# Relative attention: the placing products write PSUM in adjacent words, and ScalarE's copies of them read PSUM by a stride

## The chip, the core and the metric

The kernel is one program on one core of a Trainium2 chip. The core has five engines with queues of their own: TensorE (matrix products, shown as PE, its weight loads as PEld), VectorE (DVE), ScalarE (ACT), GpSimd (POOL) and SyncE (SP, here the main issuer of DMAs). Products land in PSUM, an accumulator memory of eight banks with 512 words of 32 bits on each of 128 partitions; everything else lies in SBUF. The metric is the device time of one execution in microseconds.

## The reference

Four blocks follow each other, each added to x (16 sequences of 256 tokens, 256 features) through a gate: causal attention, a feed-forward block with ternary weights, an attention with relative positions, and a mixture of 64 experts. The change lies in the third. Cut to it, with 16 heads of d = 16, and P = 128:

```python
qh = heads(layernorm(x) @ Wq.T + bq); kh = heads(ctx @ Wk.T + bk); vh = heads(ctx @ Wv.T + bv)
qk = einsum('bhqd,bhkd->bhqk', qh, kh)
r_k = rk_table[clip(k - q, -P, P) + P]          # one row of d for each pair (q, k)
q_rk = einsum('bhqd,qkd->bhqk', qh, r_k)
attn = softmax((qk + q_rk) / sqrt(d))
w1 = einsum('bhqk,bhkd->bhqd', attn, vh)
w2 = einsum('bhqk,qkd->bhqd', attn, r_v)        # r_v like r_k, from rv_table
x = x + tanh(g) * (rows(w1 + w2) @ Wo.T + bo)
```

The term q_rk differs for each query, so it is a product for each query over all heads, while qk is a product for each head over all queries.

## The kernel before

`relative_attention` takes four sequences at a time with all their heads (64 heads in all, `BH`), in four quarters of 64 queries (`CQ`), which makes 16 half-steps. One iteration h of `run` works on two of them: the *front* of half-step h + 1 (its scores and the shift for the softmax) and the *back* of half-step h (exponentials and weighting), and for some h also the *tail* of h - 1 (adding w1 and w2, dividing, the output product) and the projection of the next two sequences. On TensorE an iteration has three stretches.

1. The **front stretch**, a loop over 16 chunks c. Each chunk has 8 **placing products** (line 1444), one for each query q: the weights are 128 columns of the table `rk6` from column j on, the moving operand is `q_now[:, :, q]`, 64 heads of one query, that lie 64 bf16 numbers apart. The output goes to one of two banks `ps_s`. In the kernel before it lands with the 8 queries of a chunk side by side for each head, so the 64 words of one product are 8 words apart. ScalarE copies a chunk's 512 words to the tile `score` (line 1315, through its view `by_query`), where a query's scores of one head stand side by side. The second chunk of a bank waits for the copy of the first (`place_copied`). After every second chunk there are 4 **spreading products** (line 1455), which lay the shift of half-step h out in `ps_t`; VectorE adds it to the scores of half-step h (line 1204, `take_shift`) and ScalarE takes their exponential (line 1302, `take_exp`). In ScalarE's queue an exponential stands behind every second copy from the fourth on, and the last two exponentials stand behind the last copy. Where the iteration has a projection, its transposes and products lie between the chunks (`project`), and ScalarE and VectorE take them out of PSUM between their own steps. Where it has a tail in this stretch (`late == 0`), the tail lies at chunks 8 to 14 and waits for GpSimd's sum of w1 and w2 (line 1098).
2. The **score stretch**, again 16 chunks: 8 scoring products for a chunk (line 1475), one for each head over 64 adjacent queries, written in adjacent words; VectorE adds them to the placed part in `score` (line 1225). Between them are the first weighting's products (line 1497), four at a time in four column tiles of the array. In the other iterations the tail lies here (`late == 1`).
3. The **key stretch**: the maximum over keys, by transposes (line 1512), and the **second weighting** (line 1524): for each query a product over all heads, with a moving operand read by stride and an output written by stride, four at a time in column tiles.

The expert block, behind it, has one more line that the prediction reads: the **map products** (line 1890), whose weights and moving operand are read by a stride of 64 bf16 numbers and whose output is written in adjacent words.

Two lines hold the access patterns in question:

```python
pe.matmul(ps_s[c % 2][:].rearrange("p (h q) -> p q h", h=BH)[:, n, :], rk6[:, j:j + P], q_now[:, :, q], ...)
act.activation(by_query[1 - par][:, c // 8, :, q0:q0 + 8], ps_s[c % 2][:].rearrange("p (h q) -> p h q", h=BH), ACT.Copy)
```

Of the kernel before, what the change touches and what calls it, by code (L numbers as in the profile page):

```python
# [11 lines left out]
ACT = mybir.ActivationFunctionType  # L12
AX = mybir.AxisListType

P = 128
# [777 lines left out]
def relative_attention(nc, x2, ctx, g_xattn, w_q, b_q, w_k, b_k, w_v, b_v, w_o, b_o, rk_t, rv_table, x3, pack, rv_ext):  # L793
# [18 lines left out]
    BH = NB * H  # L812
# [12 lines left out]
    with ExitStack() as stack:  # L825
# [4 lines left out]
        def sem(name):  # L830
            sems.append(nc.alloc_semaphore("r_" + name))
            return sems[-1]
# [8 lines left out]
        rk6 = sb("rk6", [PR, NJ], BF16)  # L841
# [28 lines left out]
        ps_s = [pb(f"ps_s{i}", [P, 512], F32) for i in range(2)]  # L870
# [15 lines left out]
        placed, place_copied, scored, added = sem("placed"), sem("place_copied"), sem("scored"), sem("added")  # L886
# [15 lines left out]
        def fill_at(c):  # L902
            if c < CH:
                return c - 2 if c >= 2 else None
            return CH - 2 + (c - CH) // 2 if c % 2 == 0 and c < CH + 8 else None
# [347 lines left out]
        def _(act):  # L1253
# [36 lines left out]
            def step(h, front, back, tail, project_next):  # L1290
                i, t = divmod(h, 4)
                u, par, late = NP * (i + 1) + t, h % 2, t // NP

                def copy_rows():
                    act.wait_ge(z_turned, START + (h - 1) + 1)
                    act.activation(attT.rearrange("p (e s q) -> p s e q", e=2, s=NB), TAIL_BANKS[late][0][:].rearrange("p (s e q) -> p s e q", s=NB, e=2),
                                   ACT.Copy).then_inc(z_copied, 1)

                def take_exp(m):
                    act.wait_ge(shifted, START + MC * h + m + 1)  # L1300
                    part = score[par][:, :, 4 * m:4 * m + 4, :].rearrange("p k h q -> p k (h q)")
                    act.activation(part, part, ACT.Exp, scale=float(DH) ** -0.5).then_inc(expd, 1)  # L1302

                if project_next:
                    act.wait_ge(projected, START + u * FILLS - PER_BATCH + QK)
                    act.dma_start(ctx_in[:], c_rows[u, 0]).then_inc(ctx_loaded, 16)
                    act.dma_start(x_in[:], x_rows[u, 0]).then_inc(x_loaded, 16)
                for c in range(CH):
                    if front:

                        act.wait_ge(placed, START + CH * (h + 1) + c + 1)
                        if c == 0 and back:
                            act.wait_ge(w2_done, START + 2 * h)
                        q0 = 8 * (c % 8)
                        act.activation(by_query[1 - par][:, c // 8, :, q0:q0 + 8],  # L1315
                                       ps_s[c % 2][:].rearrange("p (h q) -> p h q", h=BH), ACT.Copy).then_inc(place_copied, 1)
                    if back and c % 2 and c > 1:
                        take_exp(c // 2 - 1)
                    if tail and late == 0 and c == TAIL_SLOTS[0][1]:
                        copy_rows()  # L1320
                    if project_next and c >= 2:
                        project(u, fill_at(c), h + 1)
                if back:
                    take_exp(MC - 1)
                if project_next:
                    for f in range(CH - 2, FILLS):
                        project(u, f, h + 1)
                if tail and late == 1:
                    copy_rows()
                if back:  # L1330
                    for n in range(2):
                        act.wait_ge(av_done, START + 2 * h + n + 1)
                        if n == 0:
                            act.wait_ge(att_turned, START + 2 * h)
                        act.activation(avT[:, 8 * n:8 * n + 8, :].rearrange("p g q -> p (g q)"), ps_b[n][:],
                                       ACT.Copy).then_inc(av_copied, 1)
                    for n in range(2):
                        act.wait_ge(w2_done, START + 2 * h + n + 1)
                        if n == 0:
                            act.wait_ge(av_added, START + h)  # L1340
                        act.activation(w2_raw[:, :, :, 8 * n:8 * n + 8],
                                       ps_b[n][:].rearrange("p (j g q) -> p j g q", j=4, g=NG), ACT.Copy).then_inc(w2_copied, 1)

            run(step)

        @block.tensor
        def _(pe):
# [49 lines left out]
            def step(h, front, back, tail, project_next):  # L1397
# [3 lines left out]
                q_now = q6[(h + 1) % 2]  # L1401
# [29 lines left out]
                for c in range(CH):  # L1431
                    if front:

                        if c == 0:
                            for n in range(2):
                                pe.wait_ge(packed_q[n], START + 48 * (h + 1) + 48)
                        if c == 0:
                            pe.wait_ge(added, START + CH * (h + 1))
                        if c >= 2:
                            pe.wait_ge(place_copied, START + CH * (h + 1) + c - 1)  # L1440
                        for n in range(8):
                            q = 8 * (c % 8) + n
                            j = (c // 8) * P - (q_first + q) + S - 1
                            ins = pe.matmul(ps_s[c % 2][:].rearrange("p (h q) -> p q h", h=BH)[:, n, :], rk6[:, j:j + P], q_now[:, :, q],  # L1444
                                            start=True, stop=True)
                        ins.then_inc(placed, 1)
                    if back and c % 2:

                        m = c // 2
                        if m == 0:  # L1450
                            pe.wait_ge(shift_ready, START + 2 * h + 2)
                        if m >= 2:
                            pe.wait_ge(shifted, START + MC * h + m - 1)
                        for n in range(4):
                            ins = pe.matmul(ps_t[m % 2][:, n * P:(n + 1) * P],  # L1455
                                            pick_row[:, 4 * m + n:4 * m + n + 1].to_broadcast([2 * HC, P]),
                                            shift[:], start=True, stop=True)
                        ins.then_inc(spread, 1)
                    if tail and late == 0:
                        take_tail(c)  # L1460
                    if project_next and c >= 2:
                        project(u, fill_at(c), h - 1 if tail else None)
                for c in range(CH):
                    if project_next and fill_at(CH + c) is not None:
                        project(u, fill_at(CH + c))
                    if front:
# [7 lines left out]
                        for n in range(8):  # L1474
                            ins = pe.matmul(ps_s[c % 2][:, n * CQ:(n + 1) * CQ], k6[:, h0 + n, k * P:(k + 1) * P],  # L1475
                                            q_now[:, h0 + n, :], start=True, stop=True)
# [3 lines left out]
                    if back:  # L1480
# [12 lines left out]
                        for k in range(NT):  # L1493
                            for j in range(4):
                                hd = 4 * g + j
                                first = (k * BH + hd) * VC
                                ins = pe.matmul(ps_b[g // 8][32 * j:32 * j + 32, (g % 8) * CQ:(g % 8 + 1) * CQ],  # L1497
                                                v_all[:, first:first + 32], by_query[par][:, k, hd, :],
                                                start=(k == 0), stop=(k == NT - 1), skip_group_check=True,
                                                tile_position=(0, 32 * j))  # L1500
                        if g % 8 == 7:
                            ins.then_inc(av_done, 1)
                for c in range(MC):
                    if front:
# [6 lines left out]
                        for n in range(4):  # L1511
                            ins = pe.transpose(ps_t[c % 2][:, n * P:(n + 1) * P], key_max[c % 2][:, n * P:(n + 1) * P], ident[:])  # L1512
                        ins.then_inc(turned, 1)
                    if back:
# [3 lines left out]
                        for n in range(2 * c, 2 * c + 2):  # L1518
                            for k in range(NT):
                                for j in range(4):  # L1520
                                    q = NQ * j + n
                                    m = k * P + S - 1 - (back_first + q)
                                    out = ps_b[n // 8][32 * j:32 * j + 32, :].rearrange("p (j g q) -> p q g j", j=4, g=NG)[:, n % 8]
                                    ins = pe.matmul(out, rv[:, m * DH:m * DH + 32], by_query[par][:, k, :, q],  # L1524
                                                    start=(k == 0), stop=(k == NT - 1), skip_group_check=True,
                                                    tile_position=(0, 32 * j))
                        if c % 4 == 3:
                            ins.then_inc(w2_done, 1)
                if front:
# [3 lines left out]
                        .then_inc(max_turned, 1)  # L1533

            run(step)

    nc.clear_and_free_semaphores(sems)
# [602 lines left out]
```

## Time and profile before

| | us |
|---|---|
| median of 3 runs | 2696.76 (2685.21 to 2705.37) |
| the profiled execution | 2701.31 |
| its span, first to last instruction | 2699.5 |
| TensorE busy with products | 2007.7 (74%) |
| VectorE busy | 1284.3 (48%) |
| ScalarE busy | 835.6 (31%) |
| placing products, line 1444, 2048 of them | 254.7 |
| copies of them, line 1315, 256 of them | 152.8 |

The mean granted clock of TensorE was 0.809 of full speed. Busy shares are means over stages with different limits; a change inside one stage is read from that stage's own windows and timeline. Records of products are pipelined: one lasts longer than the distance to the next, so the distance between starts is the pace.

### The profile page before, as it was taken

What the parts mean: (1) busy time and instruction counts of PE and PEld (TensorE: products, weight loads), DVE (VectorE), ACT (ScalarE), POOL (GpSimd) and SP (SyncE); (2) the same over time, 40 slices, a digit from 0 to 9 for tenths busy, and PEclk for the clock granted to TensorE, in tenths of its full rate; (3) what the DMA queues carried; (4) which work ended last, traced back from release to release, by engine and by line L of the source; (5) the groups of instructions that cost most, each with busy time, mean ns of one, the idle gap of its engine ahead of it and who ended that gap; (6) DMA issues with size and microseconds to landing.
All of it is one profiled execution on the core that took longest, in us unless ns stands there. A gap on an engine that the chain in (4) does not pass through costs nothing. (4 is left out here: it accounts for less than half of the span.)

```text
span 2699.5 us, 54675 instructions
## 1 busy us (share of the span) xinstructions
PE 2007.7 (74%) x22307; PEld 1513.8 (56%) x22308; DVE 1284.3 (48%) x2419; ACT 835.6 (31%) x1484; POOL 559.6 (21%) x519
## 2 busy tenths in 40 slices
PE   4777777774677458999999999989647757776663
PEld 3545554453566346777777777777535535554442
DVE  3434444442777216666666656656437642111112
ACT  2333333331222123434443443344224531111110
POOL 1111111110000101101110110001010008888881
PEclk8889888887788767987987887777857779888985
DMA  4455445543021452232224222311012225566566
GB/s 91 84 95 90 84 87 95 93 85 85 27 70 63 130 102 45 64 65 52 64 56 80 65 60 48 57 29 29 21 51 68 68 63 130 117 128 127 127 115 194
DMA packets 272334, 216.38 MB, mean 80 GB/s; under 512 B 88740, under 2 KB 257166, under 8 KB 271616
## 3 DMA queue, kind: packets, MB, share of 16 engines
q1 hardware_dynamic: 238528, 179.01, 29.2%
q0 software_dynamic: 24576, 27.05, 6.0%
q10 hardware_dynamic: 9024, 7.35, 0.9%
q8 instruction: 156, 2.56, 0.4%
q14 instruction: 50, 0.41, 0.1%
HBM read 147.08 MB, written 72.45 MB: 81 GB/s over the span
## 5 line engine op out<-in xcount | busy, mean ns | idle before, releaser
L1444 PE MATMUL r_ps_s<-r_q,r_rk 96*128 96x64 bf16 x2048 | 254.7, 289 | 15.0 <-DMA r_q<-parts_scratch 15.0
L1444 PEld LDWEIGHTS r_ps_s<-r_q,r_rk 96*128 96x128 bf16 x2048 | 217.4, 120 | 38.2 <-issue 29.0
L1204 DVE TENSOR_TENSOR r_score<-r_score,r_ps_t 128x1024 f32<-128x1024 f32 x128 | 154.8, 1217 | 100.4 <-PE r_ps_t L1455 100.4
L1315 ACT ACTIVATE r_score<-r_ps_s 128x512 f32<-128x512 f32 x256 | 152.8, 597 | 151.1 <-PE r_ps_s L1444 150.4
L1225 DVE TENSOR_TENSOR r_score<-r_ps_s,r_score 128x512 f32<-128x512 f32 x256 | 171.5, 688 | 53.6 <-PE r_ps_s L1475 51.3
L2001 DVE TENSOR_TENSOR e_hT<-e_sil,e_ps_gu 128x256 f32<-128x256 f32 x64 | 26.9, 421 | 324.6 <-ACT e_sil L2023 324.6
L313 DVE TENSOR_REDUCE a_row_max<-a_ps_s 128x2 f32<-128x512 f32 (+1 forms) x192 | 127.6, 685 | 66.1 <-PE a_ps_s L478 59.4
L1962 POOL DMA_INDIRECT e_rows<-rows_w_scratch,k_token x128 | 135.0, 1055 | 99.5 <-DVE e_h_last L1989 60.6
L2030 ACT ACTIVATE e_y<-e_ps_y,e_rows 128x256 f32<-128x256 f32 x128 | 53.7, 471 | 326.1 <-DMA base_scratch<-e_y,k_token 167.0
L1524 PE MATMUL r_ps_b<-r_score,r_rv 128*32 128x64 f32 x4096 | 137.9, 288 | 10.9 <-issue 10.9
L1302 ACT ACTIVATE r_score<-r_score 128x1024 f32<-128x1024 f32 x128 | 134.5, 1051 | 20.2 <-DVE r_score L1204 19.6
L1098 POOL TENSOR_TENSOR r_avT<-r_avT,r_w 128x1024 f32<-128x1024 f32 x16 | 37.6, 2353 | 494.3 <-DMA r_w<-r_w_raw 494.3
L1475 PE MATMUL r_ps_s<-r_q,r_k 96*128 96x64 bf16 x2048 | 114.0, 203 | 27.3 <-DVE r_score L1225 14.2
L2068 PE MATMUL e_ps_last<-e_wd,e_h_last 128*64 128x256 f32 x128 | 44.8, 435 | 115.0 <-DVE e_h_last L2002 114.0
L399 ACT ACTIVATE a_p<-a_ps_s 128x512 f32<-128x512 f32 x192 | 106.7, 595 | 74.0 <-PE a_ps_s L524 35.4
L1524 PEld LDWEIGHTS r_ps_b<-r_score,r_rv 128*32 128x32 f32 x4096 | 105.2, 126 | 35.0 <-issue 35.0
L1242 DVE TENSOR_REDUCE r_row_max<-r_ps_t 128x4 f32<-128x512 f32 x128 | 88.5, 691 | 66.6 <-PE r_ps_t L1512 66.4
L1497 PE MATMUL r_ps_b<-r_score,r_v_all 128*32 128x64 f32 x4096 | 116.8, 239 | 0.0
L1475 PEld LDWEIGHTS r_ps_s<-r_q,r_k 96*128 96x128 bf16 x2048 | 83.8, 104 | 58.6 <-DVE r_score L1225 19.4
L478 PE MATMUL a_ps_s<-a_k,a_q 96*128 96x256 bf16 (+1 forms) x512 | 102.8, 306 | 13.2 <-DVE a_row_max L313 11.6
L786 PE MATMUL f_ps_out<-f_w_q,f_h_hi 128*128 128x256 f32 x256 | 76.6, 329 | 41.0 <-DVE f_h_lo L712 41.0
L1977 POOL DMA_INDIRECT slots_in_scratch<-e_y,k_token x64 | 102.4, 1600 | 19.6 <-issue 18.9
(295 smaller groups left out, 4277.4 us busy)
## 6 DMA issues: line engine op xcount, KB each, us to landing
a_q<-parts_scratch SPq DMA_DIRECT2D x96, 128.0 KB, 4.2
a_k<-parts_scratch SPq DMA_DIRECT2D x96, 128.0 KB, 4.3
r_q<-parts_scratch SPq DMA_DIRECT2D x96, 128.0 KB, 3.2
e_wg<-in_L_ffn_expert_wg SPq DMA_DIRECT2D x64, 128.0 KB, 2.5
e_wu<-in_L_ffn_expert_wu SPq DMA_DIRECT2D x64, 128.0 KB, 3.0
e_wd<-in_L_ffn_expert_wd SPq DMA_DIRECT2D x64, 128.0 KB, 3.4
r_k<-parts_scratch SPq DMA_DIRECT2D x4, 1536.0 KB, 14.1
rows_w_scratch<-m_row SPq DMA_DIRECT2D x8, 640.0 KB, 3.2
```

What stands on the lines that cost most here:

```text
L313: dve.tensor_reduce(row_max[:, t, h0:h0 + n], ps_s[c % 2][:].rearrange("p (h k) -> p h k", h=n), AX.X, ALU.max).then_inc(maxed, 1)
L399: act.activation(out.rearrange("p h q -> p (h q)"), ps_s[c % 2][:], ACT.Exp).then_inc(expd, 1)
L478: ins = pe.matmul(out[:, h, :], q6[par][0:PR, h0 + h, t * P:(t + 1) * P], k6[par][0:PR, h0 + h, 0:keys], start=(t == 1), stop=(t == 0), sk ...
L1204: dve.tensor_tensor(part, part, bcast(ps_t[m % 2][:], NT), ALU.add).then_inc(shifted, 1)
L1225: dve.tensor_tensor(part, ps_s[c % 2][:], part, ALU.add).then_inc(added, 1)
L1302: act.activation(part, part, ACT.Exp, scale=float(DH) ** -0.5).then_inc(expd, 1)
L1315: act.activation(by_query[1 - par][:, c // 8, :, q0:q0 + 8], ps_s[c % 2][:].rearrange("p (h q) -> p h q", h=BH), ACT.Copy).then_inc(place_ ...
L1444: ins = pe.matmul(ps_s[c % 2][:].rearrange("p (h q) -> p q h", h=BH)[:, n, :], rk6[:, j:j + P], q_now[:, :, q], start=True, stop=True)
L1475: ins = pe.matmul(ps_s[c % 2][:, n * CQ:(n + 1) * CQ], k6[:, h0 + n, k * P:(k + 1) * P], q_now[:, h0 + n, :], start=True, stop=True)
L1497: ins = pe.matmul(ps_b[g // 8][32 * j:32 * j + 32, (g % 8) * CQ:(g % 8 + 1) * CQ], v_all[:, first:first + 32], by_query[par][:, k, hd, :], ...
L1524: ins = pe.matmul(out, rv[:, m * DH:m * DH + 32], by_query[par][:, k, :, q], start=(k == 0), stop=(k == NT - 1), skip_group_check=True, ti ...
L1962: pool.indirect_dma_start(out=rows[u][:, c, :], out_offset=None, in_=rows_w, in_offset=bass.IndirectOffsetOnAxis(ap=token[:, e * C + c:e * ...
```

## The change

Inside a bank of `ps_s` the order of a placed chunk is turned: it was head by head with the 8 queries side by side, and becomes query by query with the 64 heads side by side. A placing product now writes 64 adjacent words, and ScalarE's copy reads words 64 apart (256 bytes) with its output order unchanged. The scoring products, which use the same banks later, and the second weighting stay as they are.

```diff
@@ ScalarE, front stretch
-                                       ps_s[c % 2][:].rearrange("p (h q) -> p h q", h=BH), ACT.Copy).then_inc(place_copied, 1)
+                                       ps_s[c % 2][:].rearrange("p (q h) -> p h q", h=BH), ACT.Copy).then_inc(place_copied, 1)
@@ TensorE, front stretch
-                            ins = pe.matmul(ps_s[c % 2][:].rearrange("p (h q) -> p q h", h=BH)[:, n, :], rk6[:, j:j + P], q_now[:, :, q],
+                            ins = pe.matmul(ps_s[c % 2][:, n * BH:(n + 1) * BH], rk6[:, j:j + P], q_now[:, :, q],
                                             start=True, stop=True)
```

## Rows read from the trace of the kernel before

**Rows 1.** Windows: the relative attention (columns: stretch, length, busy by engine, clock, DMA)

```profile
979.50:1903.00 923.50, 841.85 (x13210) 670.00 (x13214) 564.35 (x863) 358.57 (x592) 98.58 (x92) 0.81 0.28 57
```

**Rows 2.** Windows of front stretches: first, projection, plain, tail

```profile
979.50:1006.50 27.00, 14.35 (x128) 13.07 (x128) 0.00 (x0) 9.56 (x16) 0.00 (x0) 0.50 0.79 127
...
1332.80:1367.50 34.70, 32.47 (x231) 26.54 (x230) 17.08 (x34) 22.50 (x42) 7.63 (x8) 0.90 0.42 99
1400.80:1419.80 19.00, 19.00 (x161) 15.90 (x160) 9.12 (x9) 15.09 (x23) 3.63 (x2) 0.59 0.23 57
...
1754.20:1783.60 29.40, 25.04 (x182) 20.76 (x182) 11.07 (x14) 15.44 (x24) 3.60 (x2) 0.59 0.17 45
```

**Rows 3.** Timeline of one chunk pair in a plain front stretch

```profile
1405.37 1.94 PE L1444 MATMUL r_ps_s<-r_q,r_rk 96*128 96x64 bf16 x16
...
1407.24 0.60 PE L1455 MATMUL r_ps_t<-r_shift,r_pick_row 64*128 64x128 bf16 x4
1407.34 0.60 ACT L1315 ACTIVATE r_score<-r_ps_s 128x512 f32<-128x512 f32 x1 [0.29 <-PE r_ps_s L1444]
...
1407.77 1.94 PE L1444 MATMUL r_ps_s<-r_q,r_rk 96*128 96x64 bf16 x16
1407.84 1.05 ACT L1302 ACTIVATE r_score<-r_score 128x1024 f32<-128x1024 f32 x1
...
1408.86 0.60 ACT L1315 ACTIVATE r_score<-r_ps_s 128x512 f32<-128x512 f32 x1
```

**Rows 4.** Lines by form, TensorE and ScalarE (busy us, mean ns, idle before)

```profile
L1444 PE MATMUL r_ps_s<-r_q,r_rk 96*128 96x64 bf16 x2048 | 254.7, 289 | 15.0 <-DMA r_q<-parts_scratch 15.0
...
L1315 ACT ACTIVATE r_score<-r_ps_s 128x512 f32<-128x512 f32 x256 | 152.8, 597 | 151.1 <-PE r_ps_s L1444 150.4
L1524 PE MATMUL r_ps_b<-r_score,r_rv 128*32 128x64 f32 x4096 | 137.9, 288 | 10.9 <-issue 10.9
...
L1302 ACT ACTIVATE r_score<-r_score 128x1024 f32<-128x1024 f32 x128 | 134.5, 1051 | 20.2 <-DVE r_score L1204 19.6
L1497 PE MATMUL r_ps_b<-r_score,r_v_all 128*32 128x64 f32 x4096 | 116.8, 239 | 0.0
L1475 PE MATMUL r_ps_s<-r_q,r_k 96*128 96x64 bf16 x2048 | 114.0, 203 | 27.3 <-DVE r_score L1225 14.2 <-DMA r_k<-parts_scratch 12.7
...
L2023 ACT ACTIVATE e_sil<-e_ps_gu 128x256 f32<-128x256 f32 x64 | 24.6, 384 | 34.3 <-PE e_ps_gu L2059 34.3
```

**Rows 5.** Lines by form, VectorE: a strided read and a plain pass

```profile
L1731 DVE TENSOR_REDUCE m_recent<-m_mask 128x64 f32<-128x256 bf16 x8 | 4.7, 593 | 0.0
...
L1708 DVE TENSOR_SCALAR m_logit<-m_ps_lp 128x256 f32<-128x256 f32 x8 | 3.3, 415 | 6.4 <-PE m_ps_lp L1847 6.4
```

**Rows 6.** Windows of the placing products alone, at either clock

```profile
1400.80:1402.60 1.80, 1.80 (x16) 1.62 (x16) 1.00 0.09 18
1407.80:1409.60 1.80, 1.80 (x16) 1.64 (x16) 0.50 0.12 27
```

**Rows 7.** Windows of the map products alone, at either clock

```profile
2203.60:2206.10 2.50, 2.50 (x120) 2.50 (x124) 0.50 0.33 116
2206.40:2208.90 2.50, 2.50 (x124) 2.50 (x116) 1.00 0.18 59
```

**Rows 8.** Timeline of TensorE: the first weighting at either clock

```profile
1420.35 0.66 PE L1497 MATMUL r_ps_b<-r_score,r_v_all 128*32 128x64 f32 x16
...
1429.06 0.43 PE L1497 MATMUL r_ps_b<-r_score,r_v_all 128*32 128x64 f32 x16
```

**Rows 9.** Windows of all engines at these two times (clock behind POOL)

```profile
1420.30:1420.90 0.60, 0.60 (x19) 0.42 (x16) 0.60 (x1) 0.60 (x1) 0.00 (x0) 0.50 0.00 0
1429.10:1429.40 0.30, 0.30 (x18) 0.23 (x16) 0.22 (x2) 0.30 (x1) 0.00 (x0) 1.00 0.00 0
```

**Rows 10.** TensorE's waits in the relative attention

```profile
PE r_ps_s L1475 <- DMA r_k<-parts_scratch: 12.7, 1, 12.7
...
PE r_ps_b L1415 <- POOL r_avT L1098: 8.7, 3, 4.4
```

## The prediction

> **What bounds the kernel now.** I first look for the stage that the edit lies in. The windows view gives the relative attention 923.5 us of the 2699.5, with TensorE busy in 841.85 of them and ScalarE in 358.57 [rows 1]. The placing products (L1444) run in its front stretches, sixteen in all, one for each front half-step. Both edited lines lie in these, so the next view is one window for each kind of stretch [rows 2]. There are four kinds. The very first (27.0 us) has no other work beside it. Six carry a projection of the next sequences (31.4 to 36.0 us; the one shown 34.7). Seven have neither a projection nor a tail (18.8 to 19.0 us; the one shown 19.00, TensorE busy in every microsecond of it). Two have a tail alone (28.5 and 29.4 us). The timeline of one pair of chunks in the third kind then shows what is late [rows 3]: TensorE starts 16 placing products at 1405.37, four spreading products at 1407.24 and the next 16 at 1407.77, so a pair takes 2.40 us without a gap on TensorE. ScalarE does two copies and one exponential in it, and stands idle 0.29 us ahead of the second copy. So TensorE sets the pair, with ScalarE close behind; VectorE has half of the stretch free (busy 9.12 of 19.00 us [rows 2]).
>
> How much room ScalarE has comes from the same rows. Its instructions overlap a little: a copy of 0.60 us is followed 0.50 us after its start (1407.34 to 1407.84), an exponential of 1.05 us 1.02 us after its start (1407.84 to 1408.86). A chunk that starts at 1407.77 has its copy started at 1408.86, 1.09 us later. In a stretch, 15 copies and 6 exponentials stand before the last copy starts (the exponentials of a chunk pair run one pair late, the last two behind the last copy). If ScalarE alone set the pace, that would be 1.09 + 15 x 0.50 + 6 x 1.02 = 14.7 us, against the 19.0 of TensorE. Reckoned back, copies can grow until 1.09 + 15 x (d - 0.10) + 6.12 = 19.0, that is to d = 0.89 us from 0.597 [rows 4], before they set this kind of stretch.
>
> **What the change does, part by part.** No instruction, wait, DMA or semaphore is added, removed or moved; only two access patterns in PSUM change. 2048 products write 64 adjacent words in place of 64 words that lie 8 words apart, and 256 copies read words 64 apart in place of adjacent ones. Their output in SBUF keeps its order.
>
> *The products.* They start 16 in 1.87 us, 0.117 us each [rows 3]. The scoring products (L1475) have the same shape, with adjacent words on both sides, and take 114.0 us for 2048, 56 ns each, against 254.7 and 124 [rows 4]. So something in the placing products costs 68 ns each. Three things differ: the weights start at odd places of a table, the moving operand is read by a stride of 128 bytes (q_now[:, :, q]), and the output is written by a stride. The change takes away the third alone. What tells them apart:
> - The second weighting (L1524) also reads its moving operand and writes PSUM by stride, but has 32 adjacent weights like the first weighting (L1497); it takes 137.9 us against 116.8 [rows 4]. So odd weights are not needed for a loss, but this row doesn't part the read from the write.
> - The map products of the next stage (L1890) do. They read moving operand and weights by a stride of 128 bytes and write PSUM in adjacent words, half as many columns as L1497. In 2.5 us there are 120 of them at clock 0.50 and 124 at clock 1.00, 20 to 21 ns each at either [rows 7]. The first weighting, with nothing strided, follows the clock: 16 in 0.66 us at a clock of 0.50, 0.43 at 1.00 [rows 8, 9]. A strided read of SBUF alone therefore makes TensorE's pace independent of its clock, as it is in L1444. (What stays open is whether the strided weights do it here, which L1444 doesn't have, or the strided operand, which it has.)
> - VectorE shows a price for the same kind of read: a reduction that reads 256 elements by a stride of 128 bytes takes 593 ns, a plain pass over 256 elements 415 [rows 5]. That is 0.70 ns an element more, on an engine that has nothing to do with TensorE's clock.
>
> So the strided read is enough to explain the placing products' pace, and it stays. Bounds for the gain: 0 (the read sets the pace), and 68 ns each, down to the scoring products. A loss is out: nothing is added on TensorE. I take 0, by the nearest rows, L1890's and the reduction's.
>
> *The copies.* No row shows ScalarE reading PSUM, or anything, by such a stride. Its own pace bounds the price from below: 384 ns for 256 and 597 for 512 elements [rows 4], 0.83 ns an element and 171 ns fixed; from SBUF it is the same (1024 elements in 1051 ns), so a changed read can't gain. From above, two rows on hops give an estimate each: VectorE's 0.70 ns more an element makes 597 + 512 x 0.70 = 0.95 us, and TensorE's placing pace of 117 ns for 64 elements, 1.83 ns each, makes 171 + 512 x 1.83 = 1.11 us. I take 597 with no conviction: all rows on hops are reads of SBUF, and none on PSUM. But up to 0.89 us the third kind of stretch does not notice, and there the cover is the 4.3 us between 14.7 and 19.0. In the first stretch placing ends in any case before the keys land (12.7 us of waiting for that DMA), and in the two stretches with a tail TensorE waits 8.7 us in all for GpSimd's sum [rows 10]; in the six with a projection ScalarE is busy for 22.50 of 34.70 us [rows 2], so 16 x 0.29 = 4.6 us more have room, if the projection's own chain through ScalarE does not lengthen. What a longer copy holds up, when it does, is the queue behind it on ScalarE: the exponentials, and in six stretches the projection's copies, for which TensorE and VectorE wait.
>
> **The sum.** 0 from the products, 0 from the copies: the profiled execution stays at 2701.3 us (span 2699.5). It stood 4.5 us over the median of the three runs, so the forecast is 2697.
>
> **Rivals.**
> *A, faster: the write was the brake.* For it: placing and second weighting share it. Against it: L1890. Then TensorE drops below ScalarE, and the seven plain stretches come down only to 14.7 us: 7 x 4.3 = 30. The six with a projection, where TensorE is busy in 32.47 of 34.70 us, gain at most 16 chunks x (0.93 - 0.45) = 8, I take 5: 30. (A chunk is 8 products: 0.93 us at 117 ns, 0.45 at 56.) The two with a tail gain on the 7 chunks behind the wait, 7 x 0.48, 3 each: 6. 2697 - 66 = 2631. The Trainium skill (PSUM — Partial Sum Buffer, Specifications (TRN2)) says that PSUM has cachelines of 8 bytes and that any non-contiguous access slows matmuls significantly; by that rule this rival is what happens. No run here shows a strided write with an adjacent read, so the rule stands untested, and L1890 shows only that it is not needed.
>
> *B, slower: the copies' strided read costs what it costs from SBUF.* A copy of 1.03 us, between the two estimates, starts its follower 0.93 later; a plain stretch takes 1.09 + 15 x 0.93 + 6.12 = 21.2 us, 2.2 more, 15 in seven. In the six with a projection the 16 x 0.43 = 6.9 us of longer copies lie partly in idle time; between 0 and 6.9 each, I take 1.5: 9. The two with a tail 0.5 each. 2697 + 25 = 2722. At 0.95 us a plain stretch takes 20.0 and the six nothing: 2704. At 1.11 us it takes 22.4 and the six up to 8.2 each: 2770. It decides from a copy of 0.89 us on. For it: both engines that hop in SBUF pay. Against it: PSUM is another memory, and it takes 64 adjacent words from TensorE in 56 ns, faster than ScalarE asks for them. The Trainium skill (Advanced Engine Details and Errata, PSUM Cachelines) asks that every two consecutive elements be adjacent for the best throughput, which speaks against a copy that never has two; no row here shows it for ScalarE.
>
> *C, both or dearer:* A's gain eaten by B's copies (plain stretches at 21.2 us although TensorE has time, the projection stretches shorter: 2697 + 15 - 30 = 2682 to 2712), or a hop dearer than either estimate: a copy of 1.45 us makes a plain stretch 27.5, 60 us more in seven, near 2760 without the six.
>
> **How the numbers follow.** Nothing that counts: 0.48, in 2686 to 2708 by the spread of the runs shown. B: 0.33. A: 0.12. C: 0.07. One per cent, 27 us, is about what a measurement of this kernel can tell from no change. B straddles that line (2704 to 2770, the line at 2724), so I give 0.20 of it to slower, the longer arm, and 0.13 to within. C gives 0.05 to slower and 0.02 to within. Slower is 0.25; faster is A, 0.12; within is 0.48 + 0.13 + 0.02 = 0.63. The range leaves out A (0.12) and the top of B and C (some 0.08): 2682 to 2750.
>
> **What the changed profile would show.** Right: L1444 still 16 in about 1.87 us, at either clock; L1315 below 0.89 us; the plain stretches at 18.8 to 19.0. A: L1444's busy time near the 114 of L1475, TensorE waiting for ScalarE's copies. B: L1315 between 0.95 and 1.11 us, idle time ahead of L1444 released by L1315, plain stretches near 21.2. The forecast is wrong if a hop in PSUM has a price of its own that SBUF rows can't show.

## The result and the profile after

The changed kernel takes 2714.79 us (median of 17 runs, 2706.31 to 2726.68) against 2694.93 of the kernel before on the same chips (17 runs): a ratio of 1.0073, 95% interval 1.0059 to 1.0087. That is 19.9 us slower, inside the range forecast and within 1%, but not nothing. The profiled execution took 2723.16 us with a mean granted clock of 0.787, against 2701.31 and 0.809 before.

Both edited lines kept their prices. The view by lines and forms of the kernel after has the rows that answer to [rows 4] (busy us, mean ns, idle before):

```profile
L1444 PE MATMUL r_ps_s<-r_q,r_rk 96*128 96x64 bf16 x2048 | 255.1, 288 | 14.9 <-DMA r_q<-parts_scratch 14.9
L1524 PE MATMUL r_ps_b<-r_score,r_rv 128*32 128x64 f32 x4096 | 138.0, 288 | 11.4 <-issue 11.4
L1497 PE MATMUL r_ps_b<-r_score,r_v_all 128*32 128x64 f32 x4096 | 121.9, 247 | 0.0
L1475 PE MATMUL r_ps_s<-r_q,r_k 96*128 96x64 bf16 x2048 | 119.3, 208 | 25.6 <-DMA r_k<-parts_scratch 12.8 <-DVE r_score L1225 12.3
...
L1315 ACT ACTIVATE r_score<-r_ps_s 128x512 f32<-128x512 f32 x256 | 152.9, 597 | 153.9 <-PE r_ps_s L1444 153.4
```

The placing products (L1444) and their copies (L1315) stand where they stood. What grew are lines that the change does not touch, in the same number of products: the projection's (L1379, two forms) by 11.0 us in all, the scoring products (L1475) and the first weighting (L1497) by 5 us each. The projection's lines, before and then after:

```profile
L1379 PE MATMUL r_ps_proj<-r_xT,r_wq_dh 128*128 128x256 f32 x128 | 45.9, 510 | 2.2 <-ACT r_xT L1276 2.2
L1379 PE MATMUL r_ps_proj<-r_cT,r_wk_dh 128*128 128x256 f32 x128 | 38.7, 429 | 0.6 <-DVE r_rest L1162 0.4
...
L1379 PE MATMUL r_ps_proj<-r_xT,r_wq_dh 128*128 128x256 f32 x128 | 53.0, 573 | 1.9 <-ACT r_xT L1276 1.9
L1379 PE MATMUL r_ps_proj<-r_cT,r_wk_dh 128*128 128x256 f32 x128 | 42.6, 466 | 0.4 <-DVE r_rest L1162 0.4
```

All of these follow TensorE's clock. At the median, projection products start 216 ns apart at a granted clock of 1.00 and 427 at 0.50, scoring products 29 and 53, the same in both kernels; for the first weighting see [rows 8, 9]. So what changed is how long each level lasted, and the next view is the windows by stretch, whose last three columns are the granted clock, the DMA share and GB/s. After, a projection stretch, a plain stretch, a stretch with a tail alone and the score stretch behind it:

```profile
1098.10:1134.19 36.09, 34.99 (x229) 28.63 (x229) 17.05 (x34) 22.71 (x42) 7.71 (x8) 0.76 0.42 95
1468.60:1487.61 19.01, 19.01 (x162) 15.92 (x161) 9.11 (x9) 15.10 (x23) 2.37 (x1) 0.56 0.44 69
...
1763.60:1793.27 29.67, 24.92 (x181) 20.75 (x181) 11.07 (x14) 15.46 (x24) 3.61 (x2) 0.60 0.18 45
1793.27:1812.11 18.84, 17.31 (x387) 13.28 (x385) 12.94 (x19) 3.57 (x5) 0.00 (x0) 0.55 0.07 17
```

The plain and the tail-only stretch are as before [rows 2]. The score stretch of the last row had this form before:

```profile
1783.56:1796.66 13.10, 11.35 (x387) 8.95 (x385) 12.78 (x19) 3.58 (x5) 0.00 (x0) 1.00 0.11 24
```

There VectorE was busy nearly throughout (12.78 of 13.10 us); after, TensorE at half clock sets it. Cutting both traces at the first placing and the first scoring product of each half-step gives the whole bill: the six projection stretches take 215.0 us against 203.8, the two score stretches behind the tail-only ones 37.9 against 26.2, and the relative attention, from its first placing to its last weighting product, 990.2 against 968.0. These two places hold 22.9 us, all of the 22.2.

One projection stretch cut where its clock changes shows how. Windows of before (the same stretch of both kernels, the second of the six):

```profile
1094.01:1100.31 6.30, 5.06 (x45) 4.14 (x45) 2.93 (x8) 2.81 (x6) 0.00 (x0) 1.00 0.35 106
1100.31:1107.11 6.80, 6.32 (x38) 4.92 (x37) 3.11 (x5) 4.64 (x9) 1.89 (x2) 0.50 0.18 41
1107.11:1127.77 20.66, 20.59 (x150) 17.38 (x148) 11.02 (x22) 14.99 (x28) 5.82 (x7) 1.00 0.53 119
```

and of after:

```profile
1098.10:1102.40 4.30, 3.23 (x29) 2.64 (x28) 1.79 (x3) 1.97 (x4) 0.00 (x0) 1.00 0.51 144
1102.40:1119.40 17.00, 16.97 (x96) 13.37 (x96) 7.42 (x15) 9.99 (x19) 5.66 (x5) 0.50 0.33 77
1119.40:1134.19 14.79, 14.79 (x107) 12.63 (x105) 7.84 (x16) 10.76 (x20) 2.05 (x3) 1.00 0.49 101
```

The clock falls to its lower level 4.3 us into the stretch in place of 6.3, and stays there for 17.0 us in place of 6.8. TensorE's busy time grows by 3.0 us (31.97 to 34.99), 0.7 of which go into its idle time, and the stretch is 2.3 us longer. TensorE's timeline in these spells shows which work pays. Before, at 1.00:

```profile
1108.50 1.13 PE L1379 MATMUL r_ps_proj<-r_xT,r_wq_dh 128*128 128x256 f32 x4
1109.47 1.06 PE L1444 MATMUL r_ps_s<-r_q,r_rk 96*128 96x64 bf16 x8
```

After, at 0.50:

```profile
1109.34 2.08 PE L1379 MATMUL r_ps_proj<-r_xT,r_wq_dh 128*128 128x256 f32 x4
1111.21 1.08 PE L1444 MATMUL r_ps_s<-r_q,r_rk 96*128 96x64 bf16 x8
```

Four projection products take twice the time, eight placing products the same. So the placing products, whose pace does not follow the clock, lose nothing by the lower clock; what stands beside and behind them does.

### The profile page after: what moved, and what is told of

It reads as the page before. It is cut to its first block and busy times, and to the rows that moved or that the text cites. A ratio compares the mean times of both kernels' runs of the same rounds, so it can differ in the third digit from the quotient of the medians.

```text
span 2721.4 us, 54676 instructions
## 1 busy us (share of the span) xinstructions
PE 2043.0 (75%) x22308; PEld 1539.4 (57%) x22308; DVE 1284.5 (47%) x2419; ACT 837.0 (31%) x1484; POOL 560.2 (21%) x519
## 5 line engine op out<-in xcount | busy, mean ns | idle before, releaser
L1444 PE MATMUL r_ps_s<-r_q,r_rk 96*128 96x64 bf16 x2048 | 255.1, 288 | 14.9 <-DMA r_q<-parts_scratch 14.9
L1444 PEld LDWEIGHTS r_ps_s<-r_q,r_rk 96*128 96x128 bf16 x2048 | 219.3, 121 | 41.4 <-issue 33.1
L1315 ACT ACTIVATE r_score<-r_ps_s 128x512 f32<-128x512 f32 x256 | 152.9, 597 | 153.9 <-PE r_ps_s L1444 153.4
L1524 PE MATMUL r_ps_b<-r_score,r_rv 128*32 128x64 f32 x4096 | 138.0, 288 | 11.4 <-issue 11.4
L1475 PE MATMUL r_ps_s<-r_q,r_k 96*128 96x64 bf16 x2048 | 119.3, 208 | 25.6 <-DMA r_k<-parts_scratch 12.8
L1524 PEld LDWEIGHTS r_ps_b<-r_score,r_rv 128*32 128x32 f32 x4096 | 105.2, 127 | 36.4 <-issue 36.4
L1497 PE MATMUL r_ps_b<-r_score,r_v_all 128*32 128x64 f32 x4096 | 121.9, 247 | 0.0
L1475 PEld LDWEIGHTS r_ps_s<-r_q,r_k 96*128 96x128 bf16 x2048 | 88.2, 107 | 58.8 <-DVE r_score L1225 17.5
```

What stands on the lines that cost most here:

```text
L1444: ins = pe.matmul(ps_s[c % 2][:, n * BH:(n + 1) * BH], rk6[:, j:j + P], q_now[:, :, q], start=True, stop=True)
```

## The experiments

All ratios are against the kernel before on the same chip. Where a line is not shown, it is that of the changed kernel (or of the kernel before, if that is named). "Plain", "projection" and "tail-only" are the kinds of front stretch. The clocks of the six projection stretches stand in order. Times of stretches and clocks are those of one profiled execution each, the ratios those of all runs.

| run | placing write | projection, us in all | their clocks | score stretches behind the tail-only ones | ratio [interval] |
|---|---|---|---|---|---|
| before | stride | 203.8 | .76 .90 .90 .90 .90 .81 | 26.2 | 1 |
| read strided alone | stride | 202.9 | .76 .90 .95 .86 .90 .90 | 26.2 | 0.9999 [0.9983, 1.0015] |
| adjacent in plain alone | by kind | 202.9 | .77 .90 .90 .86 .90 .90 | 26.2 | 1.0011 [0.9997, 1.0025] |
| after | adjacent | 215.0 | .65 .76 .76 .80 .73 .72 | 37.9 | 1.0073 [1.0059, 1.0087] |
| write adjacent alone | adjacent | 214.0 | .65 .80 .76 .81 .73 .72 | 37.4 | 1.0082 [1.0059, 1.0105] |
| adjacent in projection and tail | by kind | 211.9 | .65 .76 .76 .81 .76 .75 | 37.5 | 1.0067 [1.0042, 1.0092] |
| pairs | pairs | 214.5 | .65 .80 .81 .72 .73 .72 | 26.2 | 1.0064 [1.0041, 1.0086] |

**The two halves of the change.** In the first of these runs the products write adjacent words and ScalarE reads adjacent words, in the second both go by stride.

```diff
@@ write adjacent alone (against after)
-  ps_s[c % 2][:].rearrange("p (q h) -> p h q", h=BH), ACT.Copy)
+  ps_s[c % 2][:].rearrange("p (h q) -> p h q", h=BH), ACT.Copy)
@@ read strided alone (against before)
-  ps_s[c % 2][:].rearrange("p (h q) -> p h q", h=BH), ACT.Copy)
+  ps_s[c % 2][:].rearrange("p (q h) -> p h q", h=BH), ACT.Copy)
```

> The placing products write adjacent words as in the changed kernel, ScalarE's copies read adjacent words as in the kernel before (the scores of a chunk then land in another order in SBUF, so the output is another one; every instruction has its old size). Theory 'clock': the write pattern has no price on TensorE (16 placing products still in 1.87 us) but lets the granted clock fall in the front stretches, so this is as slow as the changed kernel: ratio 1.006 to 1.009, mean clock near 0.79. Theory 'copies': ScalarE's strided read disturbs something that its own duration doesn't show; then this equals the kernel before, ratio 0.998 to 1.002, clock near 0.81.

> The placing products write by stride as in the kernel before, ScalarE's copies read by stride as in the changed kernel (order in SBUF and so the output differ). Theory 'clock': equals the kernel before, ratio 0.998 to 1.002, copies at 597 ns, clock near 0.81. Theory 'copies': ratio 1.006 to 1.009.

The write alone gave the whole loss, the read alone nothing: 2711.57 us (1.0082) and 2689.04 (0.9999). Lines by form of the second:

```profile
L1315 ACT ACTIVATE r_score<-r_ps_s 128x512 f32<-128x512 f32 x256 | 152.9, 597 | 150.5 <-PE r_ps_s L1444 149.8
```

A ScalarE copy that reads PSUM 64 words apart takes 597 ns, like one that reads adjacent words. So the loss is the write's, with ScalarE's pattern out of it. Windows of the first run, a projection stretch and a score stretch behind a tail-only one, show it at the same places as in the changed kernel:

```profile
1091.91:1126.45 34.54, 34.04 (x230) 27.94 (x229) 17.17 (x34) 22.68 (x42) 7.66 (x8) 0.80 0.43 99
1779.83:1798.44 18.61, 17.08 (x386) 13.09 (x385) 12.85 (x19) 3.57 (x5) 0.00 (x0) 0.56 0.07 17
```

**The operand made adjacent, under either write.** The moving operand takes one head's 64 queries, which lie side by side, in place of one query's 64 heads.

```diff
@@ with the adjacent write of after; and with the strided write of before
-  rk6[:, j:j + P], q_now[:, :, q],
+  rk6[:, j:j + P], q_now[:, q, :],
```

> The changed kernel, but a placing product's moving operand is 64 adjacent numbers (all queries of one head in place of all heads of one query, so it multiplies other numbers). Theory 'the strided read of SBUF paces the placing products': they fall from 117 ns to that of the scoring products, 29 to 56 ns by the clock, plain front stretches come down from 19.0 to the 14.7 us that ScalarE needs, and the kernel by 50 to 80 us, ratio 0.970 to 0.982. Rival 'weights at odd places pace them': they stay at 117 ns, ratio 0.995 to 1.01.

> The kernel before, but with the moving operand adjacent (other numbers, as in the run beside it): the strided write by itself. Theory 'the write has a price of its own, hidden under the read': between 56 and 117 ns a product, ratio 0.97 to 0.995. Rival 'a write by stride is free on TensorE': the same pace as with both adjacent, 29 to 56 ns, ratio 0.970 to 0.982. If the write alone paces them too: 117 ns, ratio near 1.

The times were 2664.55 us (0.9897, 0.9868 to 0.9926) and 2673.23 (0.9927, 0.9902 to 0.9951). TensorE's timeline has 16 products in a row at a granted clock of 1.00 and at 0.50 (the clock as in the windows of those microseconds). Adjacent operand, adjacent write:

```profile
1155.17 0.64 PE L1444 MATMUL r_ps_s<-r_q,r_rk 96*128 96x64 bf16 x16
...
1163.12 1.09 PE L1444 MATMUL r_ps_s<-r_q,r_rk 96*128 96x64 bf16 x16 [0.29 <-ACT r_score L1315]
```

Adjacent operand, strided write:

```profile
1157.55 1.07 PE L1444 MATMUL r_ps_s<-r_q,r_rk 96*128 96x64 bf16 x16
...
1167.87 1.89 PE L1444 MATMUL r_ps_s<-r_q,r_rk 96*128 96x64 bf16 x16
```

and the windows around these two, for the clock:

```profile
1157.50:1160.00 2.50, 2.50 (x40) 2.12 (x39) 1.58 (x3) 1.78 (x4) 0.00 (x0) 1.00 0.07 13
...
1167.00:1171.00 4.00, 4.00 (x36) 3.17 (x34) 1.89 (x2) 3.94 (x7) 0.13 (x1) 0.50 0.10 22
```

The median distances of starts, over all placing products of a trace, are 29 ns (clock 1.00) and 53 (0.50) with the adjacent write, 56 and 107 with the strided one, and 110 or 111 at either clock with the strided operand, in before and after alike. So the strided read paces the placing products, as forecast, and it hides a price of the strided write that is real: twice the time for a word, in step with the clock. That the array is slowed by any non-contiguous pattern in PSUM is what the Trainium skill says (PSUM — Partial Sum Buffer, Specifications (TRN2)); these two runs agree, 56 against 29 ns, and show that here it is covered.

The first of the two missed its expectation of 50 to 80 us: it gained 26. Four of the seven plain stretches came down to 13.71 us, near ScalarE's own pace, but the other three only to 18.1 to 18.6, as the scoring behind them waits for the keys' DMA:

```profile
1225.36 0.61 PE L1475 MATMUL r_ps_s<-r_q,r_k 96*128 96x64 bf16 x8 [4.64 <-DMA r_k<-parts_scratch]
```

And the projection stretches gained nothing: 205.6 us with clocks of .66 .75 .80 .76 .75 .71, against 207.9 and .75 .81 .85 .81 .85 .76 with the strided write.

**Pairs.** The 64 words of a product lie two and two together, with a hop of 16 between, under the strided operand (which computes the reference) and under the adjacent one. ScalarE's copy, not shown, reads accordingly.

```diff
-  ps_s[c % 2][:, n * BH:(n + 1) * BH], rk6[:, j:j + P], q_now[:, :, q],
+  ps_s[c % 2][:].rearrange("p (a q b) -> p q a b", q=8, b=2)[:, n], rk6[:, j:j + P],
+  q_now[:, :, q].rearrange("p (a b) -> p a b", b=2),   # the second run: q_now[:, q, :]
```

> The changed kernel with one difference: a placing product writes its 64 words in pairs, two adjacent words and then a hop of 16, where it wrote 64 adjacent words, and ScalarE's copy reads accordingly. The operand stays strided, so the products stay 110 ns apart at either clock by every theory. Theory 'clock' (a strided write keeps the array occupied for twice as many of its cycles and so the granted clock falls less): what decides is how fast pairs are written, which the next run measures. If pairs go at the full rate (29 ns per 64 words at full clock) this run is like the changed kernel: clock 0.785 to 0.80, ratio 1.006 to 1.009, score stretches behind the tail-only ones 18.6 to 19.1 us. If pairs go at half rate it is like the kernel before: clock 0.805 to 0.82, ratio 0.998 to 1.002, those stretches 13.1 us. Rival 'whole rows': only a product that writes one unbroken run of 64 words pays, whatever the rate; then like the kernel before in either case.

> The run before with an adjacent moving operand (another head's 64 queries in place of one query of 64 heads, so it computes other numbers): nothing hides the pace of the pair write. With an adjacent write the products stood 29 ns apart at full clock and 53 at half, with a fully strided write 56 and 107. If a hop costs one more array cycle for each word written, pairs give 42 and 80; if pairs go at full rate 29 and 53; if every write that is not one run goes at half rate 56 and 107. Ratio against the kernel before 0.988 to 0.995 by every theory, between 0.990 and 0.993 of the two runs with an adjacent operand.

With the adjacent operand pairs go as fast as one unbroken run, 29 and 53 ns (ratio 0.9905, 0.9883 to 0.9928). TensorE's timeline:

```profile
1158.61 0.64 PE L1444 MATMUL r_ps_s<-r_q,r_rk 96*128 96x64 bf16 x16
...
1166.56 1.09 PE L1444 MATMUL r_ps_s<-r_q,r_rk 96*128 96x64 bf16 x16 [0.29 <-ACT r_score L1315]
```

The Trainium skill asks for this (Advanced Engine Details and Errata, PSUM Cachelines: every two consecutive elements contiguous), and TensorE's rows agree. "Any non-contiguous pattern", above, is too wide for this case: pairs with hops between them pay nothing. ScalarE's copies in the changed kernel, 597 ns with no two words together, do not need it. With the strided operand the pair write then behaves like the change: projection stretches 214.5 us, ratio 1.0064. "Whole rows" is out: a write that hops loses as well, if it goes at the full pace. One piece differs: in this profile the score stretches behind the tail-only ones keep their clock. Windows of a projection stretch and one of those:

```profile
1092.08:1126.79 34.71, 33.96 (x230) 27.92 (x230) 17.17 (x34) 22.68 (x42) 7.65 (x8) 0.80 0.42 98
1786.43:1799.53 13.10, 11.35 (x387) 8.95 (x385) 12.79 (x19) 3.58 (x5) 0.00 (x0) 1.00 0.10 24
```

The six runs of this kernel took 2701.31 to 2705.35 us (three, the profiled one among them) and 2713.73 to 2718.86 (three). The gap is about the 11 us of that piece, so it probably comes in some executions and not in others; only profiled ones show it.

**By kind of stretch.** One run writes adjacent words in the first and the plain stretches alone, the other in the projection and tail-only ones alone; ScalarE's copies follow.

```diff
@@ in plain stretches alone; the other run has "if not (...)"
+  (ps_s[c % 2][:].rearrange("p (h q) -> p q h", h=BH)[:, n, :]
+   if project_next or (tail and late == 0) else ps_s[c % 2][:, n * BH:(n + 1) * BH])
```

> The adjacent write only in the first and the plain front stretches; in the front stretches with a projection or a tail the products write by stride and ScalarE reads adjacent words, as in the kernel before. Theory 'clock': the plain stretches took 19.0 us in both kernels, and the loss lay in the projection stretches (215.0 against 203.8 us in all) and in the score stretches behind the tail-only ones (38 against 26 us), so this run equals the kernel before: ratio 0.998 to 1.003, clock 0.80 to 0.815, projection stretches 200 to 207 us in all. Rival 'carried over': a lower clock out of the plain stretches slows what follows them as well; then half of the loss or more, 1.003 to 1.008. Rival 'everywhere': the loss follows the number of products written, 10 of 16 half-steps, 1.004 to 1.005.

> The complement of the run that wrote adjacent words in the plain stretches alone (1.0011): here only the front stretches with a projection or a tail do so, and the plain ones write by stride. If the loss lies there, the two edits add up to the change: ratio 1.005 to 1.008, projection stretches 212 to 217 us in all against 203.8 before, clock 0.785 to 0.80. Rival 'carried over' (the lower clock of the plain stretches is needed as well): 1.001 to 1.004, projection stretches 204 to 210 us.

Plain alone: 2695.25 us, 1.0011. The rest alone: 2710.48 us, 1.0067. The second holds the loss and the two add up to it (1.0073). A projection and a plain stretch of the first run:

```profile
1093.44:1127.30 33.86, 31.98 (x229) 26.45 (x229) 17.07 (x34) 22.43 (x42) 7.62 (x8) 0.90 0.42 101
1404.20:1423.23 19.03, 19.03 (x161) 15.94 (x160) 9.12 (x9) 15.12 (x23) 3.64 (x2) 0.56 0.23 57
```

and a projection stretch of the second:

```profile
1093.84:1129.43 35.59, 35.09 (x229) 28.62 (x229) 17.09 (x34) 22.73 (x42) 7.66 (x8) 0.76 0.41 96
```

In the plain stretch the clock falls too (0.56, against 0.59 [rows 2]), and it costs nothing, because nearly all its work is paced by the strided read. "Carried over" is out.

**Filler products.** Does the clock stay up if the array is given more to do under the adjacent write?

```diff
+  if project_next or (tail and late == 0):
+      pe.matmul(ps_s[c % 2][:, n * BH:(n + 1) * BH], rk6[:, j:j + P], q_now[:, q, :], start=True, stop=True)
   ins = pe.matmul(ps_s[c % 2][:, n * BH:(n + 1) * BH], rk6[:, j:j + P], q_now[:, :, q],
```

> The changed kernel, and in the front stretches with a projection or a tail alone each placing product is preceded by a filler: a product with the same weights, an adjacent operand and an adjacent write to the same 64 words, which the placing product then overwrites; the reference is computed. A filler alone took 29 ns at full clock (the run with adjacent operand and write), so filler and product together keep the array at work as long as one product with a strided write, 56 ns. Theory 'work' (the clock stays up where the array works for longer in front of the same operand reads): the granted clock of the projection stretches goes from 0.65 to 0.80 back to 0.80 to 0.90 and the score stretches behind the tail-only ones back to 13.1 us; the time also takes 0 to 53 ns for each filler, 0 to 6.8 us in a stretch, so the ratio is 1.002 to 1.015 and not the verdict. Rival 'pattern' (it is the strided write itself, by its hops, that keeps the clock up): clock 0.65 to 0.80 as in the changed kernel, ratio 1.010 to 1.020.

2720.19 us, 1.0099 (1.0078 to 1.0119). Windows of a projection stretch and of a score stretch behind a tail-only one:

```profile
1095.07:1132.95 37.88, 37.88 (x357) 33.01 (x357) 17.15 (x34) 22.50 (x42) 7.69 (x8) 0.77 0.39 91
1802.89:1815.98 13.09, 11.34 (x386) 8.94 (x385) 12.77 (x19) 3.58 (x5) 0.00 (x0) 1.00 0.11 24
```

The projection stretches had clocks of .69 .77 .74 .78 .78 .82, a little over the changed kernel's and well under the kernel before's. The score stretches behind the tail-only ones were back at 13.09 us, but the pairs had those without a filler. And filler and product together took 142 ns (the median from one filler to the next; 48 from filler to product, 94 from product to filler), not 110, so the pace was changed as well. This speaks against "work" and does not settle it.

**The second weighting.** The kernel before, with L1524 alone written in adjacent words and ScalarE's L1341 reading by stride.

```diff
-  .rearrange("p (j g q) -> p q g j", j=4, g=NG)[:, n % 8]
+  .rearrange("p (q m) -> p q m", m=BH)[:, n % 8]
```

> The kernel before with its placing products untouched; here the second weighting writes 64 adjacent words for a query where it wrote words 8 apart in 16 groups of 4, and ScalarE's two copies for a half-step read by the stride. Its operand stays strided (110 ns for four products at either clock), and a copy stays at 597 ns. Theory 'clock': the pace stays at 110 ns and the granted clock of the key stretches falls below their 0.73 to 1.0, mean clock 0.78 to 0.80, ratio 1.003 to 1.012. Rival 'already full': four column tiles at a time keep the array at work in either pattern, so nothing moves, 0.998 to 1.002. Rival 'write paces': the pace falls below 110 ns, ratio 0.985 to 0.997.

2689.10 us, 0.9987 (0.9970 to 1.0005), clock 0.814: no effect. Its products last 287 ns at the median as before, four of them start every 110 or 111 ns at either clock in both kernels, and the copies last 597. The key stretches' clocks are as in before. What this write costs by itself no run measured, so the run says that the clock does not fall with every stride that is removed, and not why.

**A version that beats both.** GpSimd lays each half-step's queries out query by query in a second tile, one half-step ahead, so the placing products read adjacent numbers; the reference is computed. The cut lines are the waits of GpSimd and TensorE, and the tiles `wq` and `wk`, which now share the space of `score`. The second run writes by stride in the projection and tail-only stretches.

```diff
+  pool.tensor_copy(q_turned_rows[:], q6[g % 2][:].rearrange("p h q -> p q h")).then_inc(q_turned, 1)
...
-  rk6[:, j:j + P], q_now[:, :, q],
+  rk6[:, j:j + P], q_turned_rows[:, q, :],
```

> The changed kernel plus a GpSimd copy for each half-step that lays the 64 queries out query by query in a second tile, so that the placing products read adjacent numbers and the reference is still computed. In the run with an adjacent operand that computed other numbers, the ratio was 0.990 and the products stood 29 to 53 ns apart in place of 110. Theory 'clock' (operand paces, write hidden): the placing products again 29 to 53 ns apart, plain stretches near 13.7 us where no transfer holds what is behind, ratio 0.988 to 0.995; GpSimd's copy of 4096 numbers about twice the 1.89 us of its copy of 2048, 4 to 8 us, and hidden, since it is done for the half-step after next. Rival 'the copy is in the way': GpSimd's copy shares a port with VectorE or comes late, TensorE waits for it at chunk 0 of a front stretch, up to 8 us in each of 16 half-steps; then 0.995 to 1.03.

> The run with the queries turned by GpSimd (0.9945), but with the strided write in the front stretches with a projection or a tail, adjacent in the plain ones. Theory 'clock': with the adjacent operand the strided write no longer hides, 56 and 107 ns for 29 and 53, 128 products in a stretch, so 3.5 to 6.9 us more of TensorE in each of 8 stretches, against a clock that goes from 0.66 to 0.80 up to 0.75 to 0.85; ratio 0.990 to 0.996, the projection stretches 203 to 211 us in all. Rival 'pace wins': the strided write costs its 3.5 to 6.9 us in full, ratio 0.998 to 1.010.

2680.38 us, 0.9945 (0.9927 to 0.9963), and 2680.80 us, 0.9950 (0.9931 to 0.9968): faster than both kernels, by half of the 1.03% that the adjacent operand gave without GpSimd's copy. The copy in the view by lines and forms of the first run:

```profile
L1092 POOL COPY r_q6t<-r_q 96x4096 bf16<-96x4096 bf16 x16 | 118.2, 7391 | 99.5 <-DMA r_q<-parts_scratch 81.9 <-PE r_ps_s L1459 17.6
```

and its windows of a projection and a plain stretch:

```profile
1096.74:1131.13 34.39, 26.63 (x230) 21.06 (x230) 16.85 (x34) 21.91 (x42) 7.63 (x8) 0.75 0.41 96
1405.34:1419.05 13.71, 10.75 (x162) 7.92 (x161) 9.23 (x10) 13.43 (x23) 1.31 (x1) 0.74 0.14 35
```

and of the second, the same projection stretch:

```profile
1097.19:1130.93 33.74, 27.83 (x229) 22.68 (x229) 16.96 (x34) 22.47 (x42) 7.66 (x8) 0.85 0.41 98
```

The plain stretch is now ScalarE's (busy 13.43 of 13.71 us). Every other one still takes 17.9 to 18.8 us, since the scoring behind it waits for the keys' DMA (4.0 us of it in the one looked at). With the strided write the clock of the projection stretches is higher here too (0.75 to 0.85, against 0.66 to 0.80), and the longer products eat just that: 204.4 us for the six stretches against 204.6. Part of what GpSimd's copy costs is shown: TensorE waits 22.2 us ahead of the first half-step in place of 14.9, as that copy can't start before the queries land.

## Why the prediction was right, and where it was not

The forecast was 2697 us with no change that counts; 2714.79 is in the range and within 1%, yet slower with an interval clear of 1. By its steps:

- *The strided read of SBUF paces the placing products and stays.* Right. 110 ns between starts at either clock in both kernels, 29 and 53 once the operand is adjacent. The prices beside it were read too close together: the 56 ns of a scoring product is busy time shared out, with the long last record of each run of eight in it; from start to start scoring products too take 29 and 53. Rival A is out for its own reason: the write's price is real (56 and 107 ns) but hidden.
- *The copies cost nothing.* Right, though taken with no conviction: 597 ns in the kernel before, in the changed kernel and in both halves of the change. Rival B, which set the upper end of the range, has no part in the loss, so that the range held the time is luck in part.
- *The plain stretches stay at 18.8 to 19.0.* Right (18.83 to 19.04), and the reckoning of ScalarE's own pace, 14.7 us, was near: 13.7 where TensorE no longer sets it.
- *"A loss is out: nothing is added on TensorE."* This is the step that failed. Nothing was added, but the granted clock was taken as given. The term of the products, 0, was worth +19.9 us: about 11 in the projection stretches and 11 to 12, in the executions that have it, in the two score stretches behind the tail-only ones. [Rows 2] had the projection stretch at a clock of 0.90 with TensorE busy in 32.47 of 34.70 us; a column that could move stood there, with work of its own beside the placing products that follows it.

What is shown: the loss comes with the placing products' write alone, in the stretches where clock-following work stands beside or behind them, and with the granted clock, which is lower for every write of theirs that goes at the full pace (adjacent, pairs) and higher for the one at half pace. In the profiled executions the six projection stretches take 211.9 to 215.0 us with the first kind (four kernels) and 201.5 to 203.8 with the second (four kernels, the one with the second weighting changed among them). With the adjacent operand the clock is the same way round, but there the longer products eat the gain. For other products it is not shown: the second weighting's write moved no clock. What is open: why the half-paced write keeps the clock up. The filler run was meant to tell the array's work from the pattern, and did not settle it.

## What to carry to other kernels

Ahead of an edit that takes work off an operation that something else paces, look at which neighbours follow TensorE's clock, and read the granted clock of their windows as a term of the sum, with a sign. Before mending a stride, find which of the strides sets the pace by making each adjacent alone; here the operand's was worth 1% and the output's less than nothing. Where an output must be strided on TensorE, pairs of adjacent words give the full pace; whether the clock then holds is another matter, for here pairs lost as adjacent words did.

## What the runs showed of the hardware

- TensorE writes 64 words to PSUM in 29 ns (clock 1.00) and 53 (0.50) if they are adjacent or lie in pairs 16 words apart, in 56 and 107 if each stands alone, 8 words apart.
- TensorE reads a moving operand whose 64 bf16 numbers lie 128 bytes apart in 110 ns at either clock, that is 1.7 ns a number.
- ScalarE reads PSUM words that lie 64 apart at the pace of adjacent words (597 ns for 512 on each partition).
- The granted clock of a stretch can depend on the pattern of a write that does not set the pace: 0.90 against 0.76 in the same projection stretch, by 6.8 and 17.0 us at the lower level.
- GpSimd's strided copy of 4096 numbers on each of 96 partitions takes 7.39 us, and a VectorE maximum of 512 elements that fell beside one took 3.60 us, where its like took 0.69 in the run with an adjacent operand and no such copy. The timeline of both engines in the run with the queries turned, where VectorE's instruction ends just behind GpSimd's:

```profile
1015.23 7.15 POOL L1092 COPY r_q6t<-r_q 96x4096 bf16<-96x4096 bf16 x1 [27.40 <-DMA r_q<-parts_scratch]
...
1019.33 3.60 DVE L1249 TENSOR_TENSOR r_cT<-r_score 128x512 f32<-128x512 f32 x1
```

  It is no single case. In that run four of these maxima, both inputs of which lie in SBUF, fell beside a GpSimd copy; they took 1.06 to 3.60 us, and each ended 0.55 or 0.56 us behind the copy. The additions beside the same copies (L1239, one input in PSUM) stayed at 0.68 to 0.69. The kernel before has one such maximum too, beside GpSimd's copy of the values:

```profile
1736.83 1.89 POOL L1094 COPY r_v_all<-r_v_new 128x2048 f32<-128x2048 f32 x1 [15.11 <-issue]
1737.05 2.22 DVE L1235 TENSOR_TENSOR r_cT<-r_score 128x512 f32<-128x512 f32 x1
```
